# Edge convolution on one core: node keys compared in SBUF, per-node sums in narrow matmuls, 26 picked steps

## What is computed

```python
xn = (x - mean) * rsqrt(var + eps) * gamma + beta
xi, xj = xn[dst], xn[src]
feat = concatenate([xi, xj - xi], axis=-1)       # 200000 x 128
h = relu(feat @ W1 + b1)                          # 128 hidden
msg = h @ W2 + b2                                 # 64
agg = segment_max(msg, dst, num_segments=6250)    # empty node: 0
out = layernorm(x + relu(agg))
```

## Time and profile before

| | |
|---|---|
| median of 3 runs | 1803.86 us (1803.62 to 1804.23) |
| the profiled execution's own time | 1801.84 us |
| its span, first to last instruction | 1800.1 us |
| mean granted TensorE clock over the span | 0.977 |
| busy: PE, POOL, ACT, DVE | 1721.3, 1317.6, 939.6, 1197.9 us |
| one-hots and indirect gathers in the loop | 1176 and 1372 |

### The profile page before, as it was taken

The page is one execution under the profiler, slowest core; times in us unless marked ns, Lnnn a source line. Parts: engine busy times, 40 slices in busy tenths (PEclk is TensorE's granted clock), DMA queues, the critical chain, the costliest instruction groups (busy, mean ns, idle before and its releaser), DMA issues.

```text
span 1800.1 us, 26957 instructions
## 1 busy us (share of the span) xinstructions
PE 1721.3 (96%) x9871; PEld 851.8 (47%) x9871; DVE 1197.9 (67%) x1951; ACT 939.6 (52%) x1111; POOL 1317.6 (73%) x1388
## 2 busy tenths in 40 slices
PE   4489999999999999999999999999999999999995
PEld 3244444444444444444444444444445445444442
DVE  5556676666766766667667667676676676666753
ACT  4545555545455545555555555555555555555553
POOL 7777777777777777777777777777777777777722
PEclk8589999999999999999999999999999999999998
DMA  7633343334334333343343333343333433343320
GB/s 180 176 94 93 67 98 88 75 82 96 79 82 97 72 96 79 86 96 67 85 94 96 83 82 93 73 95 70 97 89 65 104 83 85 79 99 81 70 55 5
DMA packets 131566, 156.85 MB, mean 87 GB/s; under 512 B 74988, under 2 KB 76969, under 8 KB 131400
## 3 DMA queue, kind: packets, MB, share of 16 engines
q1 hardware_dynamic: 85674, 109.73, 19.6%
q0 software_dynamic: 44464, 45.18, 17.0%
q10 hardware_dynamic: 1294, 0.20, 0.1%
HBM read 147.24 MB, written 9.39 MB: 87 GB/s over the span
## 4 chain that ended last, share of the span: by engine, by line
PE 94%; DVE 2%; SPq 1%; DMA 1%; ACT 1%; ACTq 1%; issue 0%; POOLq 0%; POOL 0%; DVEq 0%
PE ps_g L1074 29%; PE ps_g L1081 15%; PE ps_acc L1149 11%; PE ps_mr L1118 11%; PE ps_h L1140 10%; PE ps_mr L1124 5%; PE ps_h L1133 5%; PE ps_x L1110 4%; PE ps_h L1138 2%; DMA src_t<-in_src 1%; DMA a_dram<-oh 1%; DVE runmax L939 0%; PE ps_x L1037 0%; SPq L336 0%; SPq L351 0%
## 5 line engine op out<-in xcount | busy, mean ns | idle before, releaser
L473 POOL DMA_INDIRECT xs<-in_x,src_ix x1372 | 1304.8, 951 | 420.4 <-issue 417.3
L865 DVE TENSOR_SCALAR oh<-ps_k 128x1024 bf16<-128x1024 bf16 x1176 | 731.9, 679 | 0.8
L1074 PE MATMUL ps_g<-oh,xtab 128*128 128x512 bf16 x2352 | 541.1, 380 | 0.0
L635 ACT ACTIVATE rows<-ps_mr 128x512 f32<-128x512 f32 x196 | 116.8, 596 | 554.5 <-PE ps_mr L1124 545.1
L939 DVE TENSOR_TENSOR_SCAN runmax<-rb,runmax,ps_mr 128x512 f32<-128x512 bf16 x196 | 250.6, 1278 | 181.2 <-PE ps_mr L1118 180.3
L1074 PEld LDWEIGHTS ps_g<-oh,xtab 128*128 128x128 bf16 x2352 | 217.0, 98 | 301.9 <-issue 68.9
L640 ACT ACTIVATE hid<-ps_h,bias 128x1024 f32<-128x1024 f32 x196 | 218.2, 1113 | 175.0 <-PE ps_h L1140 139.1
L1081 PE MATMUL ps_g<-oh,xtab 128*64 128x512 bf16 x2352 | 289.7, 383 | 0.0
L922 DVE TENSOR_TENSOR best<-ps_acc,last_key 128x336 f32<-128x336 f32 x196 | 99.5, 508 | 282.0 <-PE ps_mr L1124 264.2
L1149 PEld LDWEIGHTS ps_acc<-rows,best 128*106 128x106 f32 x1568 | 183.0, 172 | 160.1 <-issue 155.8
L596 ACT ACTIVATE best<-best,ones 126x1024 bf16<-126x1024 bf16 x196 | 225.1, 1149 | 6.4
(11 more groups left out here) (162 smaller groups left out, 584.6 us busy)
## 6 DMA issues: line engine op xcount, KB each, us to landing
kb<-keys_dram SPq DMA_DIRECT2D x98, 504.0 KB
rb<-reset_dram SPq DMA_DIRECT2D x98, 256.0 KB
xs<-in_x,src_ix POOLq DMA_INDIRECT x1372
src_t<-in_src SPq DMA_DIRECT2D x48, 256.0 KB, 6.7
aw<-a_dram SPq DMA_DIRECT2D x196, 31.5 KB
a_dram<-oh SPq DMA_DIRECT2D x6, 672.0 KB, 3.9
xwin<-xp_dram SPq DMA_DIRECT2D x196, 10.5 KB
out<-y SPq DMA_DIRECT2D x182, 10.5 KB
```

The costliest lines, as they stand in the source:

```text
L473: pool.indirect_dma_start(xs[:, u, t, h, :], None, x[:, :], bass.IndirectOffsetOnAxis(ap=src_ix[:, b, q + t, h:h + 1], axis=0))\
L865: dve.tensor_scalar(oh[0:PN, n % NOH, :], node_keys_ps, n % TN + 0.5, None, ALU.is_equal).then_inc(oh_ready, 1)
L1074: last = pe.matmul(ps_g[:, h, :], xtab[0:PN, t, 0:2, :].rearrange("p w c -> p (w c)"), oh[0:PN, n % NOH, h * GE:(h + 1) * GE], start=t == ...
```

## The change

1. The node keys stay in SBUF. `node_key` becomes two tiles that take turns, `take_nodes` and its copy to PSUM go, and the comparison reads SBUF. ACT may write the keys of picked step m once the one-hots of step m-2 are done.
2. `sums_of` makes one product for each half: eight calls of 42 stationary and 65 moving columns in place of four of 106 and 129 (as instructions 16 in place of 8). Half h writes partitions h*64 onward of `ps_acc`. Seven windows fit in the bank, so `add_bias` runs once a group, on 448 columns. A memset of the bank is added ahead of the loop, one of `pick` is dropped.
3. PICKED is 26: 1274 one-hots, 170 gathered steps with 1356 gathers.

```diff
-    PICKED = 24
+    PICKED = 26
...
-        rows = sb("rows", [P, 2, TG, NR])
+        rows = sb("rows", [P, 2, TG * 2, C1])
...
-        node_key = best[0:PN, 0:GE].bitcast(bf16)
+        node_key = [best[0:PN, 0:GE].bitcast(bf16), best[0:PN, 9 * GE:10 * GE].bitcast(bf16)]
...
-        node_keys_ps = ps_k[0:PN, :].bitcast(bf16)
...
             def node_keys(m):
                 act.wait_ge(src_b_in, 32 * m + 32)
-                if m > 0:
-                    act.wait_ge(node_ps, m)
-                act.activation(node_key, src_b, ACT.Identity, bias=node0[0:PN, :]).then_inc(node_key_ready, 1)
+                if m > 1:
+                    act.wait_ge(oh_ready, (m - 1) * TN)
+                act.activation(node_key[m % 2], src_b, ACT.Identity, bias=node0[0:PN, :]).then_inc(node_key_ready, 1)
...
+            chain(dve.memset(ps_acc[:, 0:GE - SL], 0.0))
             chain(dve.tensor_copy(slots_ps, slot_row[:, :]))
...
-                def take_nodes(m):
-                    dve.wait_ge(node_key_ready, m + 1)
-                    if m > 0:
-                        dve.wait_ge(oh_ready, m * TN)
-                    dve.tensor_copy(ps_k[0:PN, :], node_key.bitcast(f32)).then_inc(node_ps, 1)
-                    dve.wait_ge(node_ps, m + 1)
...
                 def node_onehot(n):
                     if n % TN == 0:
-                        take_nodes(n // TN)
-                    dve.tensor_scalar(oh[0:PN, n % NOH, :], node_keys_ps, n % TN + 0.5, None, ALU.is_equal).then_inc(oh_ready, 1)
...
+                        dve.wait_ge(node_key_ready, n // TN + 1)
+                    dve.tensor_scalar(oh[0:PN, n % NOH, :], node_key[n // TN % 2], n % TN + 0.5, None, ALU.is_equal).then_inc(oh_ready, 1)
...
-                    for p0, p1 in ((0, 64), (64, ROWS)):
-                        dve.tensor_tensor(sums[p0:p1, c0:c1, :], acc_v[p0:p1, :, p0:p0 + C], bias2[p0:p1, c0:c1, :], ALU.add).then_inc(added, 1)
+                    dve.wait_ge(added, n * 2 + 1)
+                    dve.tensor_tensor(sums[:, c0:c1, :], acc_v[:, c0:c1, 0:C], bias2[:, c0:c1, :], ALU.add).then_inc(added, 1)
...
                     for t in range(TG):
-                        last = pe.matmul(ps_acc[0:ROWS, q * NR:(q + 1) * NR], pick_cols[:, j % 2, t, 0:ROWS], rows[:, j % 2, t, :],
-                                         start=(i == 0 and t == 0), stop=(i == WI - 1 and t == TG - 1))
+                        for h in range(2):
+                            last = pe.matmul(ps_acc[h * 64:h * 64 + SL, p * C1:(p + 1) * C1], pick[:, j % 2, t * 2 + h, :],
+                                             rows[:, j % 2, t * 2 + h, :], start=(i == 0 and t == 0),
+                                             stop=(i == WI - 1 and t == TG - 1))
```

More of the change, by code:

```diff
@@ L62, in edge_conv_program @@
     ND = 6
-    NR = 2 * C + 1
-    CUTS = (0, 3, 5, WB)
     assert C == 64 and HID == P and S <= E < 2 * S and TILES == NB * SB and 0 < LR < TN and PN * TN <= N + SL and TN == 2 * TH - 1 and NW <= P
@@ L78, in edge_conv_program @@
     gathered = [k for k in range(NI) if k not in picked]
[L79 to L84, removed]
     ends = {w1 * WI + 2: (n, w0 % WB, w0 % WB + w1 - w0) for n, (w0, w1) in enumerate(GROUPS)}
@@ L193, in edge_conv_program @@
         xf = late[0:C, 0:2 * P]
-        node_key = best[0:PN, 0:GE].bitcast(bf16)
+        node_key = [best[0:PN, 0:GE].bitcast(bf16), best[0:PN, 9 * GE:10 * GE].bitcast(bf16)]
         xg = best[:, GE:3 * GE].rearrange("p (u e) -> p u e", u=2)
         onehot = best[0:SR, 3 * GE:5 * GE].bitcast(bf16).rearrange("p (u h e) -> p u h e", u=2, h=2)
-        pick = best[:, 5 * GE:7 * GE].rearrange("p (u n s) -> p u n s", u=2, s=64)
-        pick_cols = best[:, 5 * GE:7 * GE].rearrange("p (u t m) -> p u t m", u=2, t=TG)
+        pick = best[:, 5 * GE:5 * GE + 2 * TG * 2 * SL].rearrange("p (u n s) -> p u n s", u=2, s=SL)
         xp = best[:, 7 * GE:9 * GE].rearrange("p (h e) -> p h e", h=2)
@@ L223, in edge_conv_program @@
         ps_k = pb("ps_k", [P, GE])
+        acc_v = ps_acc[0:ROWS, 0:WB * C1].rearrange("p (w c) -> p w c", c=C1)
         slots_ps = ps_acc[:, GE - SL:GE]
@@ L268, in edge_conv_program @@
         xwin_in = sem("xwin_in")
-        src_b_in, node_key_ready, node_ps = sem("src_b_in"), sem("node_key_ready"), sem("node_ps")
+        src_b_in, node_key_ready = sem("src_b_in"), sem("node_key_ready")
         oh_ready, segment_ps = sem("oh_ready"), sem("segment_ps")
@@ L634, in take_rows @@
                     act.wait_ge(turn_ps, j + 1)
-                    act.activation(rows[:, j % 2, :, 0:2 * C], ps_mr[:, :].rearrange("p (t c) -> p t c", t=TG),
+                    act.activation(rows[:, j % 2, :, 0:C], ps_mr[:, :].rearrange("p (t c) -> p t c", c=C),
                                    ACT.Copy).then_inc(rows_sb, 1)
@@ L725, in _ @@
                 dve.tensor_copy(src_ix[:, 0, q0:q1, :], first_ix[:, q0:q1, :]).then_inc(src_ix_ready, 1)
-            dve.memset(rows[:, :, :, 2 * C:NR], 1.0).then_inc(ones_ready, 1)
+            dve.memset(rows[:, :, :, C:C1], 1.0).then_inc(ones_ready, 1)
             dve.memset(eps_col[:, :], EPS).then_inc(ones_ready, 1)
@@ L863, in node_onehot, with add_bias @@
                     if n % TN == 0:
-                        take_nodes(n // TN)
-                    dve.tensor_scalar(oh[0:PN, n % NOH, :], node_keys_ps, n % TN + 0.5, None, ALU.is_equal).then_inc(oh_ready, 1)
-                def add_bias(c0, c1):
+                        dve.wait_ge(node_key_ready, n // TN + 1)
+                    dve.tensor_scalar(oh[0:PN, n % NOH, :], node_key[n // TN % 2], n % TN + 0.5, None, ALU.is_equal).then_inc(oh_ready, 1)
+                def add_bias(n, c0, c1):
                     wn = c1 - c0
-                    acc_v = ps_acc[:, 0:wn * NR].rearrange("p (w c) -> p w c", c=NR)
-                    dve.tensor_tensor(bias2[:, c0:c1, :], acc_v[0:ROWS, :, 2 * C:NR].to_broadcast([ROWS, wn, C]),
+                    dve.tensor_tensor(bias2[:, c0:c1, :], acc_v[:, c0:c1, C:C1].to_broadcast([ROWS, wn, C]),
                                       b2b[0:ROWS, :].rearrange("p (a c) -> p a c", a=1).to_broadcast([ROWS, wn, C]),
                                       ALU.mult).then_inc(added, 1)
-                    subs[0] += 1
-                    dve.wait_ge(added, subs[0] * 3 - 2)
-                    for p0, p1 in ((0, 64), (64, ROWS)):
-                        dve.tensor_tensor(sums[p0:p1, c0:c1, :], acc_v[p0:p1, :, p0:p0 + C], bias2[p0:p1, c0:c1, :], ALU.add).then_inc(added, 1)
+                    dve.wait_ge(added, n * 2 + 1)
+                    dve.tensor_tensor(sums[:, c0:c1, :], acc_v[:, c0:c1, 0:C], bias2[:, c0:c1, :], ALU.add).then_inc(added, 1)
                 def norm_sum(n, c0, c1):
                     wn = c1 - c0
-                    dve.wait_ge(added, subs[0] * 3)
+                    dve.wait_ge(added, n * 2 + 2)
                     dve.wait_ge(xwin_in, 32 * WB * min(n + 1, NW // WB))
@@ L905, in norm_scale @@
                                       ALU.mult).then_inc(y_ready, 1)
-                chain(dve.memset(best[:, 5 * GE:7 * GE], 0.0))
-                subs = [0]
                 n = 0
@@ L916, in _ @@
                         dve.wait_ge(turn_ps, k - 1)
-                    if k in sub_ends:
-                        add_bias(*sub_ends[k])
+                    if k in ends:
+                        add_bias(*ends[k])
                     if 2 <= k <= NI + 1:
@@ L921, in _ @@
                             dve.wait_ge(last_ready, len(LAST_GROUPS))
-                        dve.tensor_tensor(pick[:, k % 2, :, 0:SL], slots_v,
+                        dve.tensor_tensor(pick[:, k % 2, :, :], slots_v,
                                           last_key[:, k - 2, :, :].rearrange("p t h -> p (t h)")
```

2 lines of the change are left out of this document (1 added, 1 removed).

## The result

| | before | changed |
|---|---|---|
| median | 1803.74 us (4 runs) | 1820.88 us (4 runs, 1818.24 to 1822.71) |
| ratio | | 1.0094 (1.0076 to 1.0111) |
| profiled execution, own time and span | 1801.84, 1800.1 | 1820.16, 1818.4 us |
| mean gather | 0.951 us | 1.009 us |
| last gather ends | 1727.8 | 1786.8 us |

The change costs 17 us, 0.9%, and the interval of the ratio leaves out 1. The forecast was 1836 us, slower by 32 us, with a range of 1780 to 1885.

The account below looks back on a forecast made before the run. PE bounded the kernel, with POOL's gathers a second chain 45 us behind. PE's chain would fall to 1740.6 us; POOL's, 1736.7 + 97 of holds = 1834, would bound, plus 2.0 gives 1836 us, range 1780 to 1885.

Parts of the forecast that it names:

- The sums: On PE, narrow sums take 0.50 us and the passage ahead shrinks: 0.65 us less a step, -127 us.
- The rival of short matmuls: PE bounds: the sums' 16 instructions cost 0.067 us each, as long as the 8 did, so 1870 us; chance 0.20.
- PE's chain: TensorE's whole chain: 1801.8 - 127 (sums) + 65.2 (98 more one-hots) + 0.6 = 1740.6 us.
- POOL's pace and two more picked steps: On POOL, 16 gathers fewer at 1.256 us each: -20.1 us, chain 1736.7 us if a gather keeps its pace.
- How short the comparison gets: On DVE, comparisons between SBUF and SBUF run at doubled rate and start 0.33 us apart, down from 0.60.
- The holds: On POOL, gathers wait for DVE's SBUF comparisons: +97 us over 1244 gathers, raising POOL's chain to 1834 us.
- per point 0.235 x 0.165, at two points: A gather's chance of meeting a comparison times its mean wait: 0.039 us a point, 0.078 us a gather.
- The first point: About 0.12 us after its start, a gather waits for DVE's operation to end; 0.039 us a gather.
- The second: A gather's later point, released 0.13 us before its end, waits for DVE likewise; another 0.039 us a gather.
- the two known points: The two moments in a gather when it needs something DVE holds; together 0.078 us a gather, +97 us.
- The signs: Profile marks expected: comparison mean near 0.42 us, gathers near 1.03, last gather's end near 1805, PE idle 80 us or more.
- The end: After the last gather: 3.4 us for its DMA to land, then 25.6 from the last `rows_across` to the end.

Follow-up runs that it names:

- h1: The changed kernel with the keys back in PSUM; narrow sums and 26 picked steps stay: 1738.44 us, 0.9637 of the kernel before.
- i1: The changed kernel with keys back in PSUM and TensorE's selecting matmuls left out but for the first and last of each picked step: 1736.58 us.
- i2: The changed kernel, keys in SBUF, with TensorE's selecting matmuls left out but for the first and last of each picked step: 1827.46 us.
- e7: The changed kernel with each comparison cut in two of 512 columns, on a slow chip: 2438.61 us, 1.0273.
- e1: The changed kernel with the keys back in PSUM, on a slow chip: 2376.33 us, 1.0112 of the kernel before there.
- e2: The kernel before with only the keys moved to SBUF, on a slow chip: 2386.8 us, 1.0127; again 2394.67 us, 1.0077.

## Why the prediction was right, and where not

- **The sums.** 0.50 us was forecast, 0.45 measured; the passage ahead went from 1.01 to 0.91. In the middle of the loop a step with eight one-hots took 9.85 us and one with seven takes 8.47; with 0.665 for the eighth the saving is 0.715 us. Over the whole program it is less: h1 has a span of 1737.9, and 1800.1 + 65.2 + 0.6 - 1737.9 = 128 us, 0.653 a step against the 0.65 forecast. The other 12 us lie at the ends, where PE waits for ACT and DVE: from the sums of step 185 to those of step 195 h1 takes 64.5 us and the kernel before 62.5, and its first sums come at 101.9 us in place of 100.5. PE isn't much above the gathers in h1: i1, bound by them, has a span of 1734.8. The rival of short matmuls has fallen: a pair of 42 and 65 columns costs 0.45 / 8 = 0.056 us, two instructions.
- **PE's chain.** 1740.6 us was forecast; h1's profiled execution took 1739.75.
- **POOL's pace and two more picked steps.** Without SBUF comparisons the last gather was forecast for 1727.8 - 20.1 = 1707.7; h1 has 1705.3.
- **How short the comparison gets.** 0.33 us apart was forecast and 0.335 is the median start to start in the changed kernel; a mean of 432 ns against "near 0.42". What was missed: a gather holds up 227 of them, and these raise the mean; the other 1047 have a mean of 415 ns.
- **The holds: near in size by luck, wrong in make-up.** +97 us was forecast, 48.5 a point; 81.5 was measured (1786.8 - 1705.3), in i1 and i2 90.7. The step that failed is "per point 0.235 x 0.165, at two points". The first point gave 37.5 us against its 48.5: 288 of 1308 gathers were held there, the runs included, a share of 0.22 against 0.235, and 248 of them waited 0.151 us against 0.165. The second gave 5.7, since there the gather has mostly come first and the comparison waits; and 41.1 us came from a case that the text had ruled out with one row, "in a run of two, it waited for the one under way". The two errors, 43 us too much at the second point and 41 too little for the runs, nearly cancelled, and nothing in the prediction made them do so. Had only the two known points held as they did, the time would have been near 1780, the edge of the stated range. A small error beside these: 60 gathers were taken as free behind the last one-hot, and it was 22.
- **The signs.** The mean gather was forecast near 1.03 us and is 1.009, its last end near 1805 and is 1786.8, PE's idle time ahead of `rows_across` at 80 us or more and is 57.6. The rest of what PE lost stands in its busy time, 20.6 us more than in h1, behind the nine falls of the clock shown above.
- **The end.** From the last gather's end the prediction took 3.4 + 25.6 = 29.0 us; it is 8.3 + 25.1 = 33.4. The rows land in time, but the steps between, now without one-hots, take 5.5 us each through ACT and DVE, and the last `rows_across` stands behind them.

The changed kernel's timeline there:

```profile
1785.86 0.94 POOL L464 DMA_INDIRECT xs<-in_x,src_ix  x1 [0.30 <-issue]
...
1792.69 1.12 PE L1104 MATMUL ps_mr<-ident,runmax 128*128 128x128 f32 x4 [0.51 <-DVE runmax L919]
...
1794.50 0.66 PE L1130 MATMUL ps_acc<-rows,best 128*42 128x65 f32 x16 [0.69 <-ACT rows L626]
...
1795.09 0.66 PE L1090 MATMUL ps_x<-ident,xs 128*128 128x128 f32 x4
```

In sum: 1836 - 2.4 (POOL's pace) - 15.5 (holds) + 4.4 (end) - 1.3 (the profiled execution is 0.7 below the median, not 2.0) = 1821.2 us, against the 1820.88 measured. These terms are differences between the same traces and must add up; that they do shows that none was left out, not that each has its cause.

## What to carry to other kernels

A faster instruction on an engine with idle time is worth nothing, and can cost a neighbour: DVE won 327 us of work here and the kernel lost 82, because comparisons that read and write SBUF held up the gathers that POOL issues. Before moving an operand to SBUF, list who else works from there at the same time, and cost each meeting from the rows of both engines, the run of operations too and not only one. Where both must run, their order counts: 30 us went by moving group-end operations behind the comparisons. But with the keys in PSUM the kernel takes 1738 us, 53 less than the better order.

## What the runs showed of the hardware that I had not expected

- A gather's two points differ in who waits. 0.12 us after its start the gather waits for a comparison under way (248 times, 0.151 us on average); all 252 gathers whose comparison had begun 0.04 us or more ahead of them waited, but only 13 of the 82 whose comparison began in their own first 0.12 us. At 0.12 ahead of its end it mostly doesn't wait: the comparison that starts 0.2 to 0.45 ahead of a gather's end is held until 0.25 after the gather's end and takes up to 0.67 us in place of 0.41. The Trainium skill ("SBUF — State Buffer", Who interferes with whom) says that the one who issues first gets the shared pair and the other blocks; the comparison's 628 ns against 406 to 414 for the three behind it agrees, and the prediction had used that rule in one direction only. The page also says that the pair is held for the whole instruction. Of the gather the trace doesn't agree: 466 comparisons started during a gather, 0.5 to 0.9 us ahead of its end, and none took over 0.43 us.
- A gather can wait through a whole run of back-to-back comparisons, 1.03 us on average over its 0.94, 1.3 where it meets the first of four, though ends of single comparisons pass in between. Where it met L875 ahead of eight halves (e7), it was 1.92 us over.
- TensorE on some chips: the same program at 2354 to 2376 us in place of 1804, with gaps of 0.3 to 1.0 us on issue between its selecting matmuls and a clock of 0.88 to 0.93. There e1, with narrow sums, was 1 to 2% slower than the kernel before, where the same kernel as h1 is 4% faster; e2, with wide sums and its keys in SBUF, was about 1% slower there too, so the sums aren't shown to be the reason. The cause is open.
